# A prefetch hint for the closing branch of every engine's loop, in a four-layer transformer kernel

## The chip, the cores and the metric

The kernel runs on one core of a Trainium2 chip. The metric is the device time of one execution in microseconds (us), as the median of several runs. The core has five instruction streams that run side by side and meet only at semaphores: TensorE (PE in the profile; PEld is its weight load and PEq or PEldq its sequencer), VectorE (DVE), ScalarE (ACT), GpSimd (POOL) and SyncE (SP), which here issues the DMAs.

## The reference

Sixteen sequences of 512 tokens with 256 features pass through four pre-normalised residual layers. Cut to what matters:

```python
x = x + linear_attention(layernorm(x))      # L0 attention, 16 heads, phi = silu + 1
x = x + ternary_ffn(layernorm(x))           # L0 FFN: 256 -> 1024 gated, 1024 -> 1024 twice, 1024 -> 256
x = x + softmax_attention(layernorm(x))     # L1 attention, one head of 256
x = x + tanh(layernorm(x) @ W @ A1 @ A2 + bias)   # L1 FFN
```

`x` has the shape (16, 512, 256) in float32.

## The kernel before

One tile is one sequence. Its work is cut into steps with short names: A steps are the first attention, B, U, G, H and W the ternary FFN in two halves of 256 tokens, C and D steps the second attention and the last layer. `PLAN` (L128) writes out by hand one period in which three tiles are under way at once: the FFN of the tile in the middle (no prefix), the C steps of the tile before (`c:`) and the A steps and first FFN half of the tile behind (`a:`, `n:`). Each step says for every engine what it does; every engine walks the same list and does its own part of each step. A step's products run on PE, and the other engines empty PSUM banks, split values in a high and a low part, normalise and apply the functions. Two rings of four PSUM banks (`ffn_fill`, `att_fill`) and some fifty semaphores tie the engines together; a wait inside the loop compares with a register that is worked out from the iteration number.

`walk` (L322) lays out the program of PE, DVE, ACT and POOL alike: `PROLOGUE` and `FIRST` as straight code, then a loop of T - 2 = 14 iterations over `BODY`, which is `PLAN`, then `LAST` and `TAIL` as straight code. The loop is opened in L332. SP has a loop of its own (L435) of T - SLOTS = 12 iterations, which stores a finished tile and loads a new one.

The last step of a period is `W1`: on PE 32 products into one bank (L892), on DVE the scaling of that bank (L585) and the sum with `x` (L588). The first step is `U0`: on PE 16 products (L798) for two banks, on ACT a silu of the first (L728), on DVE the product of both (L570) and its rounded part (L575). Behind it in the list come `CST`, the statistics of the C layer on DVE (L505 to L512) with a power on POOL (L475), `U1` to `U3`, and `G0` (L834), whose last products need what POOL makes of `U3` (L488). Then follows `T`, the transposes in L850.

The products of the FFN stand twice in PE's program, once for weights that need full precision and once for those that don't, behind a branch on a flag that is read once (L817, L819). With these weights PE jumps over the first copy each time, 26 times in a period.

Of the kernel before, what the change touches and what calls it, by code (L numbers as in the profile page):

```python
# [41 lines left out]
T = 16  # L42
# [4 lines left out]
SLOTS = 4  # L47
# [162 lines left out]
def build(nc, a):  # L210
    with ExitStack() as ctx:
# [110 lines left out]
        def walk(eng, part):  # L322

            def steps_of(steps, counts, slots):
                for step in steps:
                    part(step, counts, slots)
                    counts.ahead(step)

            beginning = Counts(phases[0])
            steps_of(PROLOGUE, beginning, {"a": 0, "n": 0})  # L330
            steps_of(FIRST, beginning, {"": 0, "a": 1, "n": 1})
            with eng.Fori(0, T - 2) as it:  # L332
                steps_of(BODY, Counts(phases[2], rate, it),
                         {"c": eng.snap(it % SLOTS), "": eng.snap((it + 1) % SLOTS),
                          "a": eng.snap((it + 2) % SLOTS), "n": eng.snap((it + 2) % SLOTS)})
            steps_of(LAST, Counts(phases[3]), {"c": (T - 2) % SLOTS, "": (T - 1) % SLOTS})
            steps_of(TAIL, Counts(phases[4]), {"c": (T - 1) % SLOTS})
# [5 lines left out]
        def wait_apart(eng, which, value):  # L343

            if isinstance(value, int):
                eng.wait_ge(which, value)
            else:
                register = eng.to_reg(value)
                eng.wait_ge(consts, 7)  # L350
                eng.wait_ge(which, register)
# [13 lines left out]
        def wait_taken(eng, c, ring, k):  # L365

            b, n = c.bank(ring, k)
            eng.wait_ge(taken[ring][b], n)
# [17 lines left out]
        def km(name):  # L386
            return a[name].rearrange("(k p) n -> p k n", p=P)

        @block.sync
        def _(sp):  # L390
            sp.dma_start(x[:, 0], x_in[0]).then_inc(x_loaded, 16)
            sp.dma_start(raw_wkv[:, :, 0:D], km("wk0T")).then_inc(a_loaded, 16)
            sp.dma_start(raw_wkv[:, :, D:2 * D], km("wv0T")).then_inc(a_loaded, 16)
            sp.dma_start(raw_wq, km("wq0T")).then_inc(a_loaded, 16)
            sp.dma_start(wo[:], km("wo0T")).then_inc(a_loaded, 16)
            sp.dma_start(rows[:, 0:5, :], a["rows"][None].broadcast_to([P, 5, D])).then_inc(small_loaded, 16)
            sp.dma_start(cols[:], a["cols"]).then_inc(small_loaded, 16)
            sp.dma_start(scales[:], a["scales"]).then_inc(small_loaded, 16)

            parts = [[("w1T", w12[:, 0]), ("w2T", w12[:, 1])], [("h1T", h1[:])], [("h2T", h2[:])], [("w3T", w3[:])]]

            def bounce(layer):
                for name, _ in parts[layer]:
                    sp.dma_start(a["scratch_" + name], a[name]).then_inc(w_bounced[layer], 16)

            def land(layer):
                sp.wait_ge(w_bounced[layer], 16 * len(parts[layer]))
                for name, tile in parts[layer]:
                    sp.dma_start(tile.bitcast(F32), a["scratch_" + name].rearrange("(k p) n -> p k n", p=P))\  # L410
                      .then_inc(w_loaded[layer], 16)

            for tile, name in ((raw_q, "L1_attn_w_q"), (raw_k, "L1_attn_w_k"), (raw_v, "L1_attn_w_v"),
                               (raw_out, "woutT"), (raw_f, "wfT"), (raw_a1, "L1_ffn_aux_weight1"),
                               (raw_a2, "L1_ffn_aux_weight2")):
                sp.dma_start(tile, km(name)).then_inc(c_loaded, 16)
            bounce(0)
            bounce(1)
            land(0)
            land(1)  # L420
            bounce(2)
            land(2)
            bounce(3)
            land(3)

            c = Counts(phases[0])
            for step in PROLOGUE:
                if step[:2] == ("FOLD", 1):
                    wait_taken(sp, c, "att_fill", 2)
                c.ahead(step)  # L430
            for t in range(1, SLOTS):
                sp.dma_start(x[:, t], x_in[t]).then_inc(x_loaded, 16)
                sp.wait_ge(x_loaded, 16 * (t + 1))

            with sp.Fori(0, T - SLOTS) as t:  # L435
                slot = sp.snap(t % SLOTS)
                sp.wait_ge(s["out_ready"], t + 1)
                sp.dma_start(x_out[t], x[:, slot]).then_inc(x_stored, 16)
                wait_apart(sp, x_stored, 16 * t + 16)
                wait_apart(sp, x_loaded, 16 * t + 16 * SLOTS)  # L440
                sp.dma_start(x[:, slot], x_in[t + SLOTS]).then_inc(x_loaded, 16)
            for t in range(T - SLOTS, T):
                sp.wait_ge(s["out_ready"], t + 1)
                sp.dma_start(x_out[t], x[:, t % SLOTS]).then_inc(x_stored, 16)
            sp.wait_ge(x_stored, 16 * T)
# [3 lines left out]
        def _(pool):  # L449
# [28 lines left out]
            def part(step, c, slots):  # L478
# [11 lines left out]
                elif kind == "CF":  # L490
# [4 lines left out]
                    last.then_inc(s["out_ready"], 1)  # L495

            walk(pool, part)

        @block.vector  # L500
        def _(dve):
# [19 lines left out]
            def part(step, c, slots):  # L521
# [183 lines left out]
                elif kind == "CHECK":  # L705
                    bank, out = filled(dve, c, "att_fill", 0)
                    dve.tensor_reduce(flag[:, j:j + 1], bank[:, 0:2 * LOOKS[j]], AX.X, ALU.add).then_inc(out, 1)

            walk(dve, part)

        @block.scalar
        def _(act):
            def part(step, c, slots):
# [68 lines left out]
                elif kind == "PREP":  # L783
                    act.wait_ge(a_loaded, 16 * 4)
                    act.activation(wkv[0][:], raw_wkv, ACT.Copy).then_inc(s["split_hi"], 1)
                    act.activation(wq[0][:], raw_wq, ACT.Copy).then_inc(s["split_hi"], 1)

            walk(act, part)

# [265 lines left out]
```

## Time and profile before

| | us |
|---|---|
| median of 3 runs | 2127.78 |
| lowest and highest | 2126.31, 2128.02 |
| span of the profiled execution, first to last instruction | 2125.2 |
| median less that span | 2.6 |
| PE busy with products | 2016.7 (95% of the span) |
| DVE busy | 1208.1 (57%) |
| ACT busy | 837.6 (39%) |
| POOL busy | 373.5 (18%) |

The profiled execution has no time of its own beside its span; what lies around the span is therefore taken from the median. Register, branch and semaphore instructions are not counted as busy. They show in the trace with a q behind the engine's name. In the chain of waits, "issue" is time in which an engine waited for nothing that the profile shows.

### The profile page before, as it was taken

Reading aid. Unit: us, or ns where it says so; the run is one execution under the profiler, and the core shown is the slowest. Engines: PE = TensorE matmul, PEld = TensorE weight load, DVE = VectorE, ACT = ScalarE, POOL = GpSimd, SP = SyncE. Lnnn points to the kernel's source line nnn. Section 1 sums busy time; section 2 is a strip of 40 time slices with the busy share of each in tenths; the row PEclk is TensorE's granted clock in tenths of the full one; section 3 lists DMA queues with packets and bytes.
Section 4 is the critical chain, followed back from the end, with each engine's and each line's share of the span. In section 5 each row is a group of like instructions: output and inputs, shape, how many; then the busy total and the mean of one; then the engine's idle time right before and its main releaser. Section 6 shows DMA issues by size and latency. Waiting matters only on the chain.

```text
span 2125.2 us, 40501 instructions
## 1 busy us (share of the span) xinstructions
PE 2016.7 (95%) x15484; PEld 1938.4 (91%) x15484; DVE 1208.1 (57%) x2880; ACT 837.6 (39%) x1538; POOL 373.5 (18%) x347
## 2 busy tenths in 40 slices
PE   6899999999999999999999999999999999999985
PEld 5899999999999999999999999998999999999985
DVE  5556656465565645656365565655656466565544
ACT  2334434344443444434344343444434344343422
POOL 1111212012121011211012121121211112121011
PEclk9999999999999999999999999999999999999997
DMA  9400000000000000000000000000000000000000
GB/s 364 181 3 3 23 3 16 9 2 22 2 23 3 2 22 3 22 3 12 12 2 22 3 22 3 2 23 2 22 3 2 23 2 12 3 12 2 2 13 10
DMA packets 24567, 48.68 MB, mean 23 GB/s; under 512 B 1152, under 2 KB 21376, under 8 KB 24064
## 3 DMA queue, kind: packets, MB, share of 16 engines
q1 hardware_dynamic: 24240, 43.41, 5.8%
q8 instruction: 317, 5.19, 1.0%
q14 instruction: 10, 0.08, 0.0%
HBM read 35.02 MB, written 19.92 MB: 26 GB/s over the span
## 4 chain that ended last, share of the span: by engine, by line
PE 80%; DVE 6%; POOL 4%; issue 4%; ACT 3%; DMA 3%; SPq 0%; DVEq 0%; POOLq 0%; ACTq 0%
PE ffn_fill L834 43%; PE att_fill L798 23%; PE ffn_fill L892 6%; PE ffn_fill L798 5%; POOL act_lo L488 3%; PE att_fill L850 2%; DVE whole L570 2%; PE att_fill L968 1%; DMA scratch_h2T<-in_h2T 1%; DMA scratch_h1T<-in_h1T 1%; POOL rstd_C L475 1%; ACT L728 1%; ACT xt_hi L719 1%; DVE st L505 1%; DVE act_hi L575 1%
## 5 line engine op out<-in xcount | busy, mean ns | idle before, releaser
L834 PE MATMUL ffn_fill<-act_hi,h 128*128 128x256 f32 x4096 | 989.6, 284 | 9.2 <-POOL act_lo L488 3.5
L834 PE MATMUL ffn_fill<-act_lo,h 128*128 128x256 f32 x4096 | 980.6, 281 | 0.0
L834 PEld LDWEIGHTS ffn_fill<-act_hi,h 128*128 128x128 f32 x4096 | 773.5, 189 | 16.6 <-POOL act_lo L488 6.9
L834 PEld LDWEIGHTS ffn_fill<-act_lo,h 128*128 128x128 f32 x4096 | 774.6, 189 | 3.7
L579 DVE CAST act_hi<-whole 128x512 fp32r<-128x512 f32 x256 | 110.0, 430 | 572.0 <-ACT whole L737 572.0
L737 ACT ACTIVATE whole<-ffn_fill,scales 128x256 f32<-128x256 f32 x512 | 215.1, 472 | 556.5 <-PE ffn_fill L834 555.6
L798 PE MATMUL ffn_fill<-half_hi,w 128*128 128x256 f32 x1024 | 264.4, 297 | 40.6 <-issue 30.6
L798 PE MATMUL ffn_fill<-half_lo,w 128*128 128x256 f32 x1024 | 257.7, 290 | 0.0
L798 PEld LDWEIGHTS ffn_fill<-half_hi,w 128*128 128x128 f32 x1024 | 202.7, 198 | 47.6 <-issue 46.4
L488 POOL TENSOR_TENSOR act_lo<-whole,act_hi 128x512 fp32r<-128x512 f32 x128 | 166.6, 1301 | 410.9 <-DVE act_hi L575 410.3
L475 POOL TENSOR_TENSOR rstd_B<-var_eps_B,minus_half 128x2 f32<-128x2 f32 x32 | 22.6, 707 | 1131.5 <-DVE var_eps_B L512 1131.5
L798 PEld LDWEIGHTS ffn_fill<-half_lo,w 128*128 128x128 f32 x1024 | 203.1, 198 | 0.0
L581 DVE TENSOR_TENSOR act_lo<-whole,act_hi 128x512 fp32r<-128x512 f32 x256 | 190.9, 746 | 8.8
L737 ACT ACT_TABLE_LOAD x92 | 118.0, 1283 | 160.5 <-PE ffn_fill L834 144.3
L728 ACT ACTIVATE gated<-ffn_fill,scales 128x256 f32<-128x256 f32 x256 | 105.9, 473 | 165.9 <-PE ffn_fill L798 164.6
L570 DVE SCALAR_TENSOR_TENSOR whole<-ffn_fill,scales,gated 128x256 f32<-128x256 f32 x256 | 111.9, 479 | 76.3 <-PE ffn_fill L798 70.9
L892 PE MATMUL ffn_fill<-w,act_hi 128*128 128x256 f32 x512 | 123.9, 285 | 0.0
L892 PE MATMUL ffn_fill<-w,act_lo 128*128 128x256 f32 x512 | 121.2, 279 | 0.0
L892 PEld LDWEIGHTS ffn_fill<-w,act_lo 128*128 128x128 f32 x512 | 96.6, 189 | 0.0
L892 PEld LDWEIGHTS ffn_fill<-w,act_hi 128*128 128x128 f32 x512 | 96.1, 188 | 0.0
L505 DVE BATCH_NORM_STATS2 st<-x 128x6 f32 (+1 forms) x256 | 91.2, 414 | 7.2 <-DMA x<-in_L_attn_x 5.6
L470 POOL TENSOR_TENSOR x<-x,rows 128x512 f32 (+1 forms) x64 | 86.3, 1367 | 20.0 <-DVE xn L518 18.0
(155 smaller groups left out, 3155.0 us busy)
## 6 DMA issues: line engine op xcount, KB each, us to landing
x<-in_L_attn_x SPq DMA_DIRECT2D x16, 512.0 KB, 4.0
out<-x SPq DMA_DIRECT2D x16, 512.0 KB, 3.0
h<-scratch_h1T SPq DMA_DIRECT2D x1, 4096.0 KB, 16.2
h<-scratch_h2T SPq DMA_DIRECT2D x1, 4096.0 KB, 14.0
w<-scratch_w1T SPq DMA_DIRECT2D x1, 1024.0 KB, 14.6
w<-scratch_w2T SPq DMA_DIRECT2D x1, 1024.0 KB, 17.3
w<-scratch_w3T SPq DMA_DIRECT2D x1, 1024.0 KB, 5.8
rows<-in_rows SPq DMA_DIRECT2D x1, 640.0 KB, 6.3
```

Source lines behind the costliest of these rows:

```text
L470: last = pool.tensor_tensor(xs[:, b:b + 2, :], xs[:, b:b + 2, :], row2(bias_row), ALU.add)
L475: pool.tensor_tensor(rstd_of[stage][:, :nb], var_eps_of[stage][:, :nb], minus_half[:, :nb], ALU.pow)\
L488: pool.tensor_tensor(act_lo[0][:, blocks], whole[:, n % WHOLES], act_hi[0][:, blocks].bitcast(F32), ALU.subtract).then_inc(s["ffn_ready"], 1)
L505: last = dve.bn_stats(st[:, b, :], xs[:, b, :])
L570: last = dve.scalar_tensor_tensor(whole[:, n % WHOLES, o, :], two(bank)[:, o, :], scales[:, 1, 2 * j + o:2 * j + o + 1], gated[:, j % 2, o ...
L579: dve.tensor_copy(act_hi[dst][:, blocks], whole[:, n % WHOLES]).then_inc(s["hi_ready"], 1)
L581: dve.tensor_tensor(act_lo[dst][:, blocks], whole[:, n % WHOLES], act_hi[dst][:, blocks].bitcast(F32), ALU.subtract).then_inc(s["ffn_ready ...
L728: last = act.activation(gated[:, j % 2, o, :], two(bank)[:, o, :], ACT.Silu, scale=scales[:, 0, 2 * j + o:2 * j + o + 1])
L737: last = act.activation(whole[:, n % WHOLES, o, :], two(bank)[:, o, :], ACT.Gelu, scale=scales[:, layer, 2 * j + o:2 * j + o + 1])
L798: last = pe.matmul(out, lhsT, rhs, start=n == 0, stop=n == len(pairs) - 1)
L834: last = pe.matmul(two(bank)[:, o, :], view(w), view(moving[:, k, :]), start=k == 0 and o == 0 and half == 0, stop=k == KH - 1 and half == ...
L892: last = pe.matmul(two(bank)[:, b, :], view(part_of[:, k, b * P:(b + 1) * P]), view(w3[:, k, :]), start=k == 0 and b == 0 and half == 0, s ...
```

## The change

Both loops are opened through a form that takes one more argument, `hint_back_edge=True`. The loops run over the same range on the same engines. At the head of each iteration every engine gets one instruction, which names that engine's loop-closing branch and says that it is likely taken. Nothing else is added, taken out or moved.

```diff
@@ walk
-            with eng.Fori(0, T - 2) as it:
+            with nc.Fori(0, T - 2, engines=[eng.engine], hint_back_edge=True) as it:
                 steps_of(BODY, Counts(phases[2], rate, it),
@@ block.sync
-            with sp.Fori(0, T - SLOTS) as t:
+            with nc.Fori(0, T - SLOTS, engines=[sp.engine], hint_back_edge=True) as t:
                 slot = sp.snap(t % SLOTS)
```

In PE's program this is all that changes. The piece is the head of its loop: the end of `FIRST`, the entry, the hint, a register operation, and the flag's branch of `U0`.

```order
 L819 UNCONDITIONAL_BRANCH
 L332 UNCONDITIONAL_BRANCH
+L332 BRANCH_PREFETCH_HINT
 L332 ISA
 L817 COMPARE_AND_BRANCH
```

The hint is the first instruction of the iteration, and everything behind it stands one instruction later. From the hint to the closing branch PE's listing has 1,772 rows, of which nearly all are products; a product is a weight load and a matmul in the trace, so that the loop is some 3,500 instructions long.

On DVE it stands in the same way at the head of the loop, behind the last instruction of `W1` in the straight code.

```order
 L588 TENSOR_TENSOR x<-x,xn_b 128x512
 L332 UNCONDITIONAL_BRANCH
+L332 BRANCH_PREFETCH_HINT
 L332 ISA
 L341 ISA
```

Here too only the hint is new. By the same listing (which leaves out waits and register moves) the loops of DVE, ACT and POOL are 229, 87 and 49 rows long.

## Rows read from the trace of the kernel before

**Rows 1.** The page: engines, and the chain that ended last, by engine

```profile
PE 2016.7 (95%) x15484; PEld 1938.4 (91%) x15484; DVE 1208.1 (57%) x2880; ACT 837.6 (39%) x1538; POOL 373.5 (18%) x347
...
PE 80%; DVE 6%; POOL 4%; issue 4%; ACT 3%; DMA 3%; SPq 0%; DVEq 0%; POOLq 0%; ACTq 0%
```

**Rows 2.** Waits of PE: total us, times, longest us

```profile
PE ffn_fill L798 <- issue: 30.6, 15, 2.6
```

**Rows 3.** The loop's own instructions: duration in ns min/median/max, first and last start

```profile
L332 ACTq COMPARE_BRANCH  x14: 40/45/45, 284.3 to 1949.2; - x14
...
L332 PEldq COMPARE_BRANCH  x14: 76/3520/3893, 286.1 to 1950.9; - x14
...
L332 DVEq COMPARE_BRANCH  x14: 50/56/68, 288.8 to 1953.7; - x14
```

**Rows 4.** The same for SP's loop

```profile
L435 SPq COMPARE_BRANCH  x12: 44/45/54, 242.0 to 1650.8; - x12
```

**Rows 5.** The same, one back edge alone, 285 to 292 us

```profile
L332 PEldq COMPARE_BRANCH  x1: 3297/3297/3297, 286.1 to 286.1; - x1
L332 DVEq ALU_OP  x1: 40/40/40, 288.7 to 288.7; - x1
L332 DVEq COMPARE_BRANCH  x1: 68/68/68, 288.8 to 288.8; - x1
L332 DVEq FUSED_REGOPS  x1: 63/63/63, 289.2 to 289.2; - x1
L332 PEldq FUSED_REGOPS  x1: 50/50/50, 289.4 to 289.4; - x1
```

**Rows 6.** DMA from 287 to 288 us: queue, packets, MB, share

```profile
q8 instruction: 1, 0.02, 6.0%
```

**Rows 7.** Chain of work, loop entered from straight code: start, us, what

```profile
159.24 3.74 PE ffn_fill L892 x32
162.98 1.90 PE ffn_fill L798 x16
...
164.91 0.02 DVEq L362
...
165.10 0.89 DVE whole L570 x2
...
174.87 1.22 PE ffn_fill L834 x8
176.08 0.87 PE att_fill L850 x8
```

**Rows 8.** Chain of work at the first back edge

```profile
287.95 1.97 issue
289.92 3.07 PE ffn_fill L798 x16
...
302.98 1.21 PE ffn_fill L834 x8
304.19 0.87 PE att_fill L850 x8
```

**Rows 9.** Chain of work, end of the last iteration, exit to straight code

```profile
1949.07 3.74 PE ffn_fill L892 x32
1952.81 1.91 PE ffn_fill L798 x16
```

**Rows 10.** Stretches: length, busy us (instructions) of PE, PEld, DVE, ACT, POOL, clock, DMA

```profile
162.98:176.08 13.10, 11.98 (x99) 11.54 (x98) 11.06 (x27) 4.64 (x9) 6.66 (x6) 1.00 0.01 3
287.95:304.19 16.24, 13.68 (x99) 13.27 (x99) 11.05 (x27) 4.65 (x9) 6.68 (x6) 0.89 0.01 3
...
289.92:295.30 5.38, 5.38 (x32) 5.38 (x33) 2.06 (x6) 1.55 (x4) 0.68 (x1) 0.68 0.01 3
```

**Rows 11.** PE's flag branches, 60 to 80 us, then 160 to 1955 us: ns min/median/max

```profile
L817 PEldq COMPARE_BRANCH  x4: 218/1757/3918, 61.5 to 75.5; - x4
...
L817 PEldq COMPARE_BRANCH  x366: 200/224/463, 161.6 to 1953.7; - x183
```

**Rows 12.** Waits of PE, 60 to 80 us: total us, times, longest us

```profile
PE ffn_fill L834 <- issue: 2.3, 2, 1.7
```

## The prediction

> **What bounds the kernel now.** I read the page first: PE is busy for 2016.7 of 2125.2 us and the chain that ended last is 80% PE [rows 1]. So a branch can only matter where PE itself runs dry. The next view is the list of PE's waits. Its longest entry is no wait for another engine but "issue", 30.6 us in 15 pieces of up to 2.6 us, ahead of the products of a U step [rows 2]. U0 is the first step of an iteration, and 14 iterations have 13 taken back edges; that fits. The third view is the loop's own line. PE's closing branch is there 14 times, with a median of 3520 ns and a minimum of 76 ns, while the same branch takes 40 to 68 ns on DVE, ACT and POOL [rows 3] and 44 to 54 ns on SP [rows 4]. The minimum is the fourteenth, which is not taken: it began at 1950.9, and behind it PE goes from W1 into the straight code with no gap, 1949.07 + 3.74 = 1952.81 [rows 9]. The thirteen taken ones are the long ones.
>
> One edge in detail shows why. PE's branch begins at 286.1 and takes 3.297 us; the next instruction is at 289.4 [rows 5]. In that time a single packet of 16 KB moves on the instruction queue, in the microsecond from 287 to 288 [rows 6]. PE still had products in its queue and finished W1 at 287.95; then it stands for 1.97 us [rows 8]. On DVE the branch takes 0.068 us and the next instruction starts 0.3 us later [rows 5], with no such fetch. So the code at the head of the loop is on DVE still at hand when the branch comes, and on PE, whose loop of 3,500 instructions is by far the longest, it has to be brought.
>
> **What an edge costs.** The loop's first iteration is entered from straight code, without a back edge, and runs the same steps; it is the measure of a free edge. From the end of W1 to the transposes behind G0 it takes 13.10 us there, 162.98 to 176.08, and 16.24 us at the first back edge, 287.95 to 304.19 [rows 7, 8]. That is 3.14 us, more than the gap of 1.97. The rest is the clock: the granted clock is 1.00 in the first stretch, and 0.68 from 289.92 to 295.30 [rows 10], that is, behind the gap PE works for a while at 1.2 instead of 2.4 GHz, and U0 takes 3.07 us instead of 1.90 [rows 7, 8]. A part of that is swallowed, since the way from U0 over DVE and POOL to G0 has some slack of its own.
>
> For all 13 I take periods, from the end of one loop-closing W1 to the next. The first is 287.95 - 162.98 = 124.97 us, without an edge in it. The 13 others, each with one taken edge at its start, take 1952.81 - 287.95 = 1664.86 us, or 128.07 each [rows 7, 8, 9]. The difference is 3.10 us per edge and 40.2 us in all.
>
> **The change, part by part.** (1) PE's hint. If it does what it says, the code at the loop's head is there when PE's sequencer reaches the branch, and the branch costs what it costs on DVE: 0.07 us and 0.3 to the next instruction. The sequencer is ahead of the array at that place: it reaches the branch at 286.1, PE finishes W1 at 287.95, a lead of 1.85 us. From the branch's end at 289.4 to the first product at 289.92 another 0.52 us pass [rows 5, 8]. So the branch and the hint behind it may together take 1.85 - 0.52 = 1.33 us before PE feels anything. Taken with 0.4 us for the branch, that leaves 0.9 us for a hint. PE then has no gap, and without a gap no slower clock, as at the loop's entry, where the clock stayed at 1.00. The term is -40.2 us.
>
> (2) The hint's own time, 14 times on each engine. No hint is in this trace. The nearest rows are the loop's register operations, 0.05 us on PE and 0.063 on DVE; the far end is the longest flag branch in the loop, 0.463 [rows 5, 11]. I take 0.05 to 0.1 us as the row of the same kind. On PE it lies under the lead just worked out. On DVE it lies ahead of U0's product: at the entry DVE took up its wait for this at 164.91, 1.93 us after the end of W1 [rows 7]; at the back edge its sequencer is through with the branch and at the next instruction at 289.2, 1.25 us after W1 [rows 5, 8]. The margin is 0.7 us, which takes either end. ACT and POOL have passed their branches 3 us and more before W1 ends [rows 3], and SP waits for a finished tile most of the time. All of these are 0; if the DVE margin were gone, each tenth beyond it would cost 1.3 us over 13 edges. Both ends for the whole: 0 and +2.
>
> (3) The loop's exit. There the hint is wrong once. If the head's code has been brought instead of the code behind the loop, PE pays one on-demand fetch, as an edge does now: 3.1 us. The other end is 0, since the branch not taken cost 76 ns and the code behind it was there [rows 3, 9]. I take 0.3.
>
> (4) Everything behind the hint stands one instruction later. The flag branches, taken 26 times in an iteration over some 32 to 64 instructions, stay under 0.463 us in the whole loop [rows 11]; one place more or less should keep it so. 0.
>
> Sum: -40.2 + 0.3, or -39.9. Against the profiled span of 2125.2 this is 2085.3. The median of the runs is 2.6 us above that span, which gives **2087.9 us**, 1.9% less. The span is one execution, and the three runs lie 1.7 us apart, so the terms are good to about 1 us plus their own bounds. The 13 edges agree well enough to be scaled: the branch's median is 3.52 and its maximum 3.89 us [rows 3]. The full case is 2084 to 2093. What is late next, once the edge is free, is the way from U0 over DVE's statistics and POOL to G0: the first iteration has it, and it is in the 124.97 us.
>
> **The rivals.** *The hint changes nothing on PE.* Between the hint and its branch lie some 3,500 instructions, many fetches of 16 KB, and 26 taken flag branches without hints. If any of these makes the fetch unit forget what it was told, or if it only ever brings what comes next, the branch stays at 3.5 us. For it speaks that nothing in this trace shows code being brought ahead of a taken branch to a far place; against it, that the branch not taken is served in 76 ns, so that fetching ahead does work along this code. Time: 2127.8, or up to 2 more. Chance 0.12. The Trainium skill, "Runtime: NRT & Kernel Launch", section on instruction fetch mechanics, calls the prefetch "purely sequential" and says that a taken branch to a target outside the two pages at hand forces a fetch before execution goes on. Its second part the trace bears out, with 3.3 to 3.9 us; by its first part the hint would be without effect, and the time this rival's.
>
> *Half a cure.* The fetch starts ahead of the branch but too late, or the hint's work itself is dear, and a part of the 3.5 us remains beyond the 1.33 that are hidden. With half of the gap left, about 1.1 us on each edge, and less of the slow clock, 15 to 20 us of the 40 stay: 2103 to 2108. Against it: while PE runs W1 alone, 3.74 us, there is more time than the branch takes now. Chance 0.10.
>
> *Slower: the hinted code takes another's place.* Room for code is limited, else PE's head would still be there. If the block that the hint brings in pushes out, or goes ahead of, the block that comes next in the body, a flag branch or a plain step inside each iteration has to wait for its code. That this costs something can be seen before the loop: two flag branches of up to 3.918 us there, with 2.3 us of issue on PE [rows 11, 12]. One such miss in each of 14 iterations at an edge's price of 3.1 us is +43. If the back edge becomes free as well, the two cancel and the time is 2131 with a wrong exit; if it does not, 2171. The point from which it decides is 13 misses: fewer, and the change gains. In the loop as it is there is no flag branch over 0.463 us, which speaks for slack in the fetches. Chance 0.07, in which the time is over 2132.
>
> **How the numbers follow.** Chances: full case 0.71, half a cure 0.10, nothing 0.12, slower 0.07. A difference of 0.2%, about 4 us, is what a measurement of this kernel can tell. Faster takes the full case and the half: 0.81. Same: 0.12. Slower: 0.07. The range has to reach from the full case through the half cure: 2083 to 2110, which leaves 0.19 out.
>
> **What would show it.** Right: PE's 13 taken closing branches at well under 1.3 us; no "issue" ahead of U0; U0 at 1.9 us and the granted clock at 1.00 behind each edge; about 125 us from W1 to W1; DVE's branch unchanged. The exit branch and what follows it show term 3. Wrong: closing branches still at 3.3 us and more (rival one), long flag branches in the body or new issue gaps ahead of L834 (rival three), or a DVE product of U0 that starts more than 2.2 us after W1 (term 2).

## The result, and the profile after

| | before | after |
|---|---|---|
| median of 20 runs each, us | 2128.12 | 2130.36 |
| lowest and highest, us | 2124.45, 2131.2 | 2126.15, 2137.27 |
| ratio, 95% interval | | 1.0013 [1.0007, 1.0019] |
| span of the profiled execution, us | 2125.2 | 2128.1 |

The change does not pay. It costs about a thousandth of the time, inside the 0.2% that the prediction called "same", and 40 us from the forecast of 2087.9. The page of the kernel after reads as before [rows 1]:

```profile
PE 2017.7 (95%) x15484; PEld 1940.3 (91%) x15484; DVE 1207.4 (57%) x2880; ACT 837.5 (39%) x1538; POOL 373.9 (18%) x347
...
PE 80%; DVE 6%; issue 4%; POOL 4%; DMA 3%; ACT 2%; SPq 0%; DVEq 0%; POOLq 0%; ACTq 0%
```

The longest wait of PE is still there, with the same count [rows 2]:

```profile
PE ffn_fill L798 <- issue: 31.5, 15, 2.6
```

The loop's own instructions (ns min/median/max, first and last start in us) show the hint on every engine, and show that PE's closing branch did not get shorter [rows 3, 4]:

```profile
L332 POOLq BRANCH_PREFETCH_HINT  x14: 31/31/43, 154.8 to 1818.3; - x14
...
L332 PEldq BRANCH_PREFETCH_HINT  x14: 45/45/45, 161.3 to 1828.3; - x14
...
L332 DVEq BRANCH_PREFETCH_HINT  x14: 39/39/61, 164.1 to 1827.5; - x14
...
L332 ACTq COMPARE_BRANCH  x14: 44/49/68, 284.5 to 1952.0; - x14
...
L332 PEldq COMPARE_BRANCH  x14: 85/3636/3803, 286.3 to 1953.8; - x14
...
L332 DVEq COMPARE_BRANCH  x14: 55/61/84, 289.0 to 1956.5; - x14
```

The chain of work at the first back edge has the same gap behind W1 [rows 8]:

```profile
284.39 3.74 PE ffn_fill L892 x32
288.13 2.44 issue
290.57 2.18 PE ffn_fill L798 x16
```

And the instruction queue, from 278.2 us to 286.2, the moment at which that branch begins (40 slices of 0.2 us, a digit where a packet starts, then the count of packets):

```profile
DMA  0000002000000000000000000000000000000000
...
q8 instruction: 1, 0.02, 0.7%
```

One fetch at 279.5, and then nothing for almost seven microseconds up to the branch. The next starts at 287.3, a microsecond into the branch, as in [rows 6]. In both kernels there are 317 fetches in all, 20 from one closing branch to the next. So the hint was executed 14 times and nothing was fetched on its account ahead of the branch.

**Where the small loss comes from.** From the end of one W1 to the next, the 13 periods with an edge take (1955.65 - 288.13) / 13 = 128.27 us, against 128.07 before: 0.20 us each, 2.6 in all. Behind a branch that is not hidden, nothing is hidden: from the hint at 290.0 to the register operation at 290.1 the sequencer needs 0.1 us more than before, while PE stands.

```profile
L332 PEldq COMPARE_BRANCH  x1: 3654/3654/3654, 286.3 to 286.3; - x1
...
L332 PEldq BRANCH_PREFETCH_HINT  x1: 45/45/45, 290.0 to 290.0; - x1
L332 PEldq FUSED_REGOPS  x1: 50/50/50, 290.1 to 290.1; - x1
```

That is 1.3 us over 13 edges, about half of the loss. The taken branches themselves, which vary between 3.3 and 3.9 us in either kernel, sum to 46.8 us here against 46.3 before, another 0.5. What is left is not assigned, and no run carries the hints of the other engines alone.

### The profile page after: what moved, and what is told of

Read it like the earlier page. It is cut to its first block, busy times and chain, and to the rows that moved or that the text cites. A ratio compares the mean times of both kernels' runs of the same rounds, so it can differ in the third digit from the quotient of the medians.

```text
span 2128.1 us, 40569 instructions
## 1 busy us (share of the span) xinstructions
PE 2017.7 (95%) x15484; PEld 1940.3 (91%) x15484; DVE 1207.4 (57%) x2880; ACT 837.5 (39%) x1538; POOL 373.9 (18%) x347
## 4 chain that ended last, share of the span: by engine, by line
PE 80%; DVE 6%; issue 4%; POOL 4%; DMA 3%; ACT 2%; SPq 0%; DVEq 0%; POOLq 0%; ACTq 0%
PE ffn_fill L834 43%; PE att_fill L798 22%; PE ffn_fill L892 6%; PE ffn_fill L798 5%; POOL act_lo L488 3%; DVE whole L570 2%; PE att_fill L850 2%; PE att_fill L968 1%; DMA scratch_h2T<-in_h2T 1%; DMA scratch_h1T<-in_h1T 1%; POOL rstd_C L475 1%; DVE st L505 1%; DVE act_hi L575 1%; ACT L728 1%; DMA h<-scratch_h2T 1%
## 5 line engine op out<-in xcount | busy, mean ns | idle before, releaser
L798 PE MATMUL ffn_fill<-half_hi,w 128*128 128x256 f32 x1024 | 266.0, 298 | 43.0 <-issue 31.5
L798 PE MATMUL ffn_fill<-half_lo,w 128*128 128x256 f32 x1024 | 259.0, 291 | 0.0
L798 PEld LDWEIGHTS ffn_fill<-half_hi,w 128*128 128x128 f32 x1024 | 203.8, 199 | 49.5 <-issue 48.7
L798 PEld LDWEIGHTS ffn_fill<-half_lo,w 128*128 128x128 f32 x1024 | 204.0, 199 | 0.0
```

What stands on the lines that cost most here:

```text
L798: last = pe.matmul(out, lhsT, rhs, start=n == 0, stop=n == len(pairs) - 1)
```

## The experiments

All full-computation kernels below differ from the kernel before only in PE's loop; those of the last group that have a hint keep the hints of the other engines as well. In the kernels whose hint does not stand at the head, the loop is written by a helper that does what `Fori` does and puts the hint where a mark stands in the code. "Fetch" means a packet of 16 KB on the instruction queue. How many instructions one brings can be read from noflag2_head below, where PE runs through all of its loop: 4,011 instructions in the trace of an iteration and 16 fetches, 251 each. It is taken as 256 instructions of 64 bytes, called a block here. By the compiled program PE's loop with its hint is 4,899 instructions from head to closing branch, 19 blocks and 35, which fits the 20 fetches of an iteration; the prediction's count of 3,500 had left out that a full-precision product is four instructions. All times are medians; "one run" means a single time. The kernel before, run beside them, gave single times from 2122.6 to 2132.1 us over all chips, so a single time can tell 40 us, barely 10, and not 3. Where a single time is all there is, the argument rests on the lengths of its 6 or 13 closing branches.

### Is the price of the edges right?

**pe_straight**: PE's 14 periods written out one behind the other, no loop on PE, the other engines keep theirs.

```diff
-            with eng.Fori(0, T - 2) as it:
-                steps_of(BODY, Counts(phases[2], rate, it),
+            straight(steps_of, phases[2], rate) if eng.engine == mybir.EngineType.PE else None
+            for it in opened(eng, T - 2): steps_of(BODY, Counts(phases[2], rate, it),
```

> PE's 14 periods written out as straight code, no loop and no back edge on PE; the other engines keep their loops. This prices the edges themselves, apart from any hint: 13 edges at 3.10 us each, so 2128.1 - 40 = 2088 (2084 to 2094), with no issue gap ahead of U0. If the code written out costs fetches of its own, or registers had hidden something, it lies above 2094.

Measured: 2086.69 us, ratio 0.9803 [0.9787, 0.982]. At the place of the first back edge U0 follows W1 at once:

```profile
284.43 3.74 PE ffn_fill L892 x32
288.17 1.90 PE ffn_fill L798 x16
```

The 13 edges cost 41 us, where the prediction had 40.2. The term was right; what failed is the hint.

### Is the hint too far ahead, or lost at a flag branch?

Between the hint at the head and its branch lie 26 taken flag branches and 19 fetches. Three kernels carry the hint nearer to the branch:

```diff
-                    emit(lambda ap: ap)
+                    mark(pe, c, "else"); emit(lambda ap: ap)
...
+PLACES = [('H', 3, 'else', 2)]
```

**h3_else** puts it into the second H3, behind that step's flag branch, with only W1's flag branch left between; **h3_ahead** ahead of H3's flag branch; **w1_else** behind W1's, with no taken branch between.

> PE's hint alone, moved from the head of the loop to the last H3 of the period, inside the copy of its products that is executed, so behind H3's own flag branch; one flag branch (W1's) and two plain branches lie between it and the closing branch. Three theories. Forgetting at any flag branch: W1's flag branch voids it, closing branches stay at 3.3 to 3.9 us and the time at 2128 to 2130, unless the fetch has already been started by then, which happens if the block that holds the closing branch is entered between the hint and W1; the last fetch ahead of the branch was 7.2 us before it, while H3 was under way, so in that case the branches fall under 0.5 us and the time to 2086 to 2092. Distance (a hint 128 us ahead of its branch is too early): the same 2086 to 2092, since 9 us are left. Hints never work on PE: 2128 to 2130, closing branches at 3.5 us.

> The same hint a few instructions earlier: directly ahead of H3's flag branch instead of directly behind it. If a flag branch voids a hint, closing branches are at 3.5 us here and the time is 2128 to 2130, whatever the run before it shows. If only distance matters, it is as good as the run before it: 2086 to 2092 and branches under 0.5 us.

> PE's hint inside the executed copy of W1, behind the last flag branch of the period, some 70 instructions and about 3 us ahead of the closing branch. No flag branch follows, so forgetting would let it work if the fetch still starts when the block is already entered: branches at 0.1 to 1.5 us, time 2086 to 2105. If the fetch unit decides only on entering a block, the hint comes too late: branches at 3.5 us, 2128 to 2130. Never: 2128 to 2130.

Measured: 2128.26 us, ratio 1.0003 [0.9994, 1.0013]; 2125.79 and 2129.4 (one run each). The closing branches, in this order:

```profile
L1089 PEldq COMPARE_BRANCH  x14: 85/3505/3736, 286.9 to 1951.4; - x14
```
```profile
L1089 PEldq COMPARE_BRANCH  x14: 85/3466/3879, 286.2 to 1949.8; - x14
```
```profile
L1089 PEldq COMPARE_BRANCH  x14: 85/3430/3836, 288.0 to 1953.6; - x14
```

None helps. Even 3.7 us ahead with nothing in between, about the time that the branch needs on demand (3.3 to 3.8 us), the hint does nothing. So it is not its distance alone, and in w1_else there was no flag branch to lose it at.

I then laid the loop's head at a fixed place, instruction 10 of a block, with the hint at H3 and without any:

```diff
+    if SLOT is not None:
+        eng.addr_align(bass.FETCH_BLOCK_INSTRUCTIONS, offset=SLOT, max_nops=0)
     nc.br(start_name, engines=engines)
```

> The hint stands behind H3's flag branch as before, but the loop's head is laid to place 10 of a block of 256 instructions, so that the block which holds the closing branch begins some 180 instructions ahead of it: behind the hint (217 ahead) and before W1's flag branch (140 ahead). Voiding theory (any flag branch that is executed makes a hint void, and the fetch unit looks at the hint when it enters a block): for the first time nothing lies between the hint and the entry, so the 13 closing branches fall from 3.5 us to under 0.5, and the time to 2086 to 2092. Theory that hints don't work on PE at all: 3.5 us and 2128 to 2130.

> The same layout with no hint anywhere: the control for the layout. Closing branches at 3.5 us, 2126 to 2130, by both theories. If the branches are short here, the layout did it and not the hint.

> The same layout with the hint directly ahead of H3's flag branch, 283 instructions before the closing branch, so well before the entry, but with one flag branch between. Voiding theory: closing branches at 3.5 us, 2128 to 2130. If what counts is only that the hint comes before the entry of the block, it is as good as behind the flag branch: 2086 to 2092.

Measured: 2126.18 us, ratio 0.9996 [0.9983, 1.0009]; 2129.26 and 2125.66 (one run each); closing branches at medians of 3.47, 3.41 and 3.53 us. The three did not separate anything. They read as if place did not matter, which was a wrong conclusion from one place only, as the last group shows.

### Does it work in another body?

**noflag2_head** has no flag branches in PE's loop (the copies of the products for weights that need full precision are left out there), two periods in an iteration and the hint at the head; **noflag2_none** is the same without the hint. Both have 6 taken back edges. Below are the line that leaves the copies out, and the one in which the two differ.

```diff
+                if c.it is not None: return emit(lambda ap: ap)
...
-PLACES, SLOT, AT_TOP = [], None, True
+PLACES, SLOT, AT_TOP = [], None, False
```

> PE's loop without flag branches (the copy of the FFN products for weights that need full precision is left out in the loop) and with two periods in an iteration, some 3,970 instructions, so that it is longer than the loop of the change; the hint stands at the head, as in the change. There are 6 taken back edges instead of 13. Voiding theory: the hint holds over 3,900 instructions and some fifteen blocks, closing branches under 0.5 us, 2086 to 2092. Distance theory or no effect on PE: six branches at 3.5 us, six edges at 3.1 us, so 2104 to 2109.

> The loop of two periods without flag branches, this time without a hint: the control for the run that came out at 2086.4 with closing branches of 0.36 us. The copy of the FFN products for weights that need full precision is left out in the loop. If the hint did the work there, the 6 taken branches are at 3.3 to 3.9 us here and the time is 2104 to 2109. If it was the shorter code or the lack of flag branches, nothing changes: 0.36 us and 2086 to 2088.

Measured, one run each: 2086.4 and 2096.55 us. The hint is worth 10 us over 6 edges, and the closing branches, with it and without:

```profile
L1093 PEldq COMPARE_BRANCH  x7: 88/357/358, 411.5 to 1907.5; - x7
```
```profile
L1093 PEldq COMPARE_BRANCH  x7: 83/3482/3890, 410.1 to 1921.2; - x7
```

So the hint does what it says, over 4,000 instructions. The control still missed its 2104 to 2109: an edge is worth less in total than the 3.1 us that the expectation took. From one closing branch to the next it is worth 2.5 us ((1921.2 - 410.1) / 6 = 251.85 against (1907.5 - 411.5) / 6 = 249.33), 15 us in all. The kernel with the hint is 1.4 us later before its first back edge and loses 3.6 us behind the loop. Of these, 1.9 us are a wait that noflag2_none does not have, four products behind the loop's exit, the one place where the hint is wrong:

```profile
1909.36 0.47 PE ffn_fill L798 x4
1909.83 1.86 issue
```

My theory was then that a flag branch on the way voids it. Three kernels tested that. **last4_h1** takes the flag branches (and the full-precision copies) out of the last four steps only, H1, H2, H3 and W1, and hints ahead of H1, so that no branch lies between; **last4_head** is the same code with the hint at the head and 22 flag branches between; **last4_w1flag_h1** hints ahead of H1 but keeps W1's flag branch.

```diff
+                if bare(c): return emit(lambda ap: ap)
...
+PLACES, SLOT, AT_TOP, BARE = [('H', 1, 'ahead', 2)], None, False, [('H', 1, 2), ('H', 2, 2), ('H', 3, 2), ('W', 1, 1)]
```

> One period per iteration and all the flag branches of the change but the last four (H1, H2, H3 in the second half and W1, whose full-precision copy is left out); PE's hint stands directly ahead of H1, about 275 instructions before the closing branch, so that no flag branch follows it and at least one block of 256 instructions is entered behind it. Voiding theory: the 13 closing branches fall to about 0.36 us, 2086 to 2092. If hints work only in a loop free of flag branches: 3.5 us and 2126 to 2130.

> The same code as the run before it with the hint at the head of the loop, as in the change, and so ahead of the 22 flag branches that are left. Voiding theory: closing branches at 3.3 to 3.9 us, 2126 to 2130. If only a flag branch close to the end or after the entry of the last block did harm: 0.36 us, 2086 to 2092.

> As the hint ahead of H1, but W1 keeps its flag branch and both copies: one flag branch between hint and closing branch. Voiding theory: 3.5 us and 2126 to 2130 if the last block is entered behind that branch, under 0.5 us and 2086 to 2092 if it is entered ahead of it and the fetch is under way. With the full-precision copy of W1 the closing branch lies 140 instructions and more behind W1's flag branch, so the place of the entry decides; a fetch in the DMA rows between 12 and 8 us before the closing branch and none 1 us after it would show the second.

Measured, one run each: 2126.1, 2101.88 and 2089.01 us. The closing branches in this order:

```profile
L1098 PEldq COMPARE_BRANCH  x14: 85/3492/3773, 286.3 to 1950.1; - x14
```
```profile
L1098 PEldq COMPARE_BRANCH  x14: 93/2116/2701, 287.7 to 1926.5; - x14
```
```profile
L1098 PEldq COMPARE_BRANCH  x14: 85/459/473, 288.1 to 1913.0; - x14
```

The theory fell, and from both sides: the kernel without a branch behind the hint fails, the ones with one and with 22 succeed in full or in part. The instruction queue shows what tells them apart. Here are the 8 us up to the first closing branch, in slices of 0.2 us, of last4_h1, last4_head and last4_w1flag_h1:

```profile
DMA  0000000000000000000000000000000000000000
```
```profile
DMA  0000000000000000000000000000000000000030
```
```profile
DMA  0000000000000000000000000400000000000000
```

No fetch: 3.5 us. A fetch 0.35 us ahead: 2.4 us left at this edge (2.1 at the median). A fetch 2.9 us ahead: 0.46 us. The branch is as long as its fetch is late: over the 13 edges of last4_head the fetch starts between 1.3 us ahead of the branch and 0.3 us behind its start, and the branch ends 2.3 to 2.9 us after the fetch starts each time, as it does where the fetch starts on demand, 1.0 us into a branch of 3.3 to 3.9. And the fetch at -2.9 us comes 1.1 us behind W1's flag branch, which in that kernel jumps to a place not entered before (it takes 0.36 us; inside the same block it takes 0.23). That led to the theory of place: **the target's fetch starts only when PE's sequencer has come into the block that holds the closing branch**, whenever the hint itself was executed. The next group bears it out where the block is entered by a jump, and leaves it open where it is entered by running on.

### The place in the block

These kernels are the change itself, whole computation, hint at the head, plus one argument that says at which instruction of a block PE's loop begins. The closing branch is 35 instructions further on in its own block.

```diff
-            with nc.Fori(0, T - 2, engines=[eng.engine], hint_back_edge=True) as it:
+            with nc.Fori(0, T - 2, engines=[eng.engine], hint_back_edge=True, head_slot={eng.engine: 100} if eng.engine == mybir.EngineType.PE else None) as it:
```

> The change as it is, whole computation, with one argument more on PE's loop: its head is laid at instruction 100 of a block of 256 instructions (the instruction queue fetches 256 instructions, 16 KB, at a time in the trace). The body is 4,899 instructions, 19 blocks and 35, so the closing branch should come near instruction 135 of its block instead of near its beginning. Theory of place (the target is fetched ahead only if the block that holds the closing branch is entered long enough before the branch): nearly all closing branches of line 332 under 0.6 us, the fetch of the target one to four us before them, and 2086 to 2092 us. Theory that something in the body that all layouts with the full-precision copy share voids the hint: branches stay at 3.3 to 3.9 us, 2125 to 2131 us.

> The same place of PE's loop head (instruction 100 of a block) without any hint. Both theories: closing branches 3.3 to 3.9 us, 2124 to 2130 us. If the place alone shortened the back edge, the branches would be short here too, and the theory of place would be about the layout and not about the hint.

> As slot100_head with the head at instruction 40, the closing branch thus near instruction 75 of its block. Theory of place: graded, the branch comes about one quarter of a block after its block is entered, so the branches lie between 0.4 and 2 us and the time between 2086 and 2110 us. Theory of something shared in the body: 3.3 to 3.9 us, 2125 to 2131 us.

> As slot100_head with the head at instruction 200, the closing branch thus near instruction 235 of its block: it is late in its block. Theory of place: under 0.6 us, 2086 to 2092 us, the fetch of the target several us ahead. Theory of something shared in the body: 3.3 to 3.9 us, 2125 to 2131 us.

> The change as it is with PE's loop head laid at instruction 10 of a block. In slot40_head and slot100_head the last flag branch of the body (line 817, ahead of W1's products) takes 0.44 us, as those do that jump into a block not entered before, and a fetch, that of the hinted target, follows it by 1.1 us, 2.8 us before the closing branch. With the head at 10 all places move back by 30, that jump should stay inside the block it comes from, and the closing branch's block is entered by running on, too late. Theory of place: branches 3.3 to 3.9 us, 2124 to 2130 us, no fetch in the five us before them. If the fixed head alone mends it (a moved label of the loader, say), 0.44 us and 2086 to 2089 us.

> The same with the head at instruction 25, fifteen instructions short of slot40_head. Theory of place: if the last flag branch still jumps into the closing branch's block, 0.44 us and 2086 to 2089 us; if it falls short of it, that block is entered by running on, and the branches lie between 1 and 3.9 us, the time between 2098 and 2130 us. In either case the length of that flag branch (0.44 or 0.23 us) and the length of the closing branch go together.

Measured (slot100_head in 4 runs, ratio 0.9818 [0.9801, 0.9835]; the others one run each):

| head at | hint | time, us | last flag branch, us | last fetch ahead of the closing branch | closing branch, median us | issue ahead of U steps (L798), us |
|---|---|---|---|---|---|---|
| 10 | yes | 2132.25 | 0.23 | 7.2 us | 3.38 | 30.1 |
| 25 | yes | 2130.62 | 0.23 | 7.2 us | 3.49 | 30.2 |
| 40 | yes | 2086.19 | 0.42 | 2.8 us | 0.44 | none listed |
| 100 | yes | 2087.35 | 0.35 | 2.9 us | 0.44 | 2.0 |
| 100 | no | 2121.21 | 0.42 | 2.9 us | 3.40 | 34.2 |
| 200 | yes | 2124.95 | 0.24 | 5.1 us | 0.45 | 27.2 |

The flag branch and the fetch are those of one edge, the third for the head at 200 and the first for the others. Of the expectations, those of slot10_head, slot25_head and slot100_none missed their times by 0.6 to 2.8 us (single times) and met their branches, slot40_head came in at the best end of a wide range, and slot200_head missed.

Fifteen instructions of padding, from 25 to 40, are worth about 44 us, one run each. The flag branch ahead of W1, the last of the body, and under it the instruction queue in the 8 us up to the first closing branch, first with the head at 25, then at 40:

```profile
L817 PEldq COMPARE_BRANCH  x1: 232/232/232, 285.4 to 285.4; - x1
```
```profile
DMA  0002000000000000000000000000000000000000
```
```profile
L817 PEldq COMPARE_BRANCH  x1: 422/422/422, 281.8 to 281.8; - x1
```
```profile
DMA  0000020000000000000000000030000000000000
```

At 25 that jump takes 0.23 us, which is read as staying in the block it comes from, and no fetch follows. At 40 it takes 0.42 us and is read as landing in the next one, the block of the closing branch. The count agrees: W1's executed copy is 64 instructions, and the closing branch stands some 60 (head at 25) or 75 (head at 40) into its block. At 40 the fetch follows 1.2 us later, 2.8 us before the closing branch, and the branch takes 0.42 us. The two go together as the expectation of slot25_head put it.

With the head at 100 the same fetch is seen with and without the hint. The 8 us up to the first closing branch, and all branches of L332, of slot100_head and then of slot100_none (15 of them, since the jump over the padding ahead of the loop is counted too):

```profile
DMA  0000200000000000000000000200000000000000
```
```profile
L332 PEldq COMPARE_BRANCH  x15: 85/441/456, 162.2 to 1910.8; - x15
```
```profile
DMA  0003000000000000000000000200000000000000
```
```profile
L332 PEldq COMPARE_BRANCH  x15: 76/3404/3936, 159.7 to 1945.3; - x15
```

Without the hint, what is fetched at that moment does not help the back edge; with it, the branch is short. The fetches from the first closing branch to the second show that the hint replaces one and adds none. Without it there are 21, since the target has to be fetched on demand besides; with it there are 20:

```profile
q8 instruction: 21, 0.34, 1.1%
```
```profile
q8 instruction: 20, 0.33, 1.0%
```

The reading nearest to this is that on coming into a block PE fetches one further block, the next in order, and that the hint changes which one. What a packet holds the trace does not say, so this is inferred from the lengths of the branches. The place alone does not shorten the back edge: slot100_none has all its 13 long branches. The same control for the head at 40 was not run.

**slot200_head** is the miss worth looking at. Its closing branches are short, 0.45 us, and yet it gains nothing. At the third back edge, the closing branch, the flag branch behind it, and the chain of work:

```profile
L332 PEldq COMPARE_BRANCH  x1: 447/447/447, 544.2 to 544.2; - x1
...
L332 PEldq BRANCH_PREFETCH_HINT  x1: 45/45/45, 544.7 to 544.7; - x1
```
```profile
L817 PEldq COMPARE_BRANCH  x1: 2618/2618/2618, 545.1 to 545.1; - x1
```
```profile
544.92 1.17 PE ffn_fill L892 x10
546.09 1.66 issue
547.75 2.18 PE ffn_fill L798 x16
```

The next taken branch, U0's flag branch, stands a few instructions behind the head and jumps over the full-precision copy, 16 products or some 64 instructions, out of the head's block, of which only 56 instructions were left. So the hint seems to have brought the head's block and no other. The stall has moved from the closing branch to the flag branch, 0.45 us later. From 160 to 1955 us there are 15 flag branches over a microsecond, 13 behind the back edges, one in the first iteration and one behind the exit, and none over 0.5 in the change or with the head at 40. All flag branches of that stretch, of slot200_head and of the kernel after [rows 11]:

```profile
L817 PEldq COMPARE_BRANCH  x367: 207/233/3392, 163.0 to 1952.4; - x184
```
```profile
L817 PEldq COMPARE_BRANCH  x365: 207/232/472, 161.8 to 1954.2; - x183
```

With the head at 100 it begins to show: 14 flag branches, U1's, take 0.8 to 1.7 us there, of which PE's queue covers all but the 2.0 us of the table. 40 is the better place.

## Why the prediction was wrong

**The step that failed is term (1)**, in its first sentence: "the code at the loop's head is there when PE's sequencer reaches the branch". It took for granted that a hint executed 120 us ahead is acted on in time, wherever the loop lies. In this body it was not acted on at all ahead of the branch: no fetch in the last 7 us, and the branch at 3.64 us instead of 3.52. What decides is the place of PE's loop in its blocks of 256 instructions: with the same hint the branch takes 3.4 to 3.5 us with the head at instruction 10 or 25 of a block, and 0.44 at 40 or 100. The rival "the hint changes nothing on PE" gave 2127.8 "or up to 2 more", and that is in effect what came, 2130.36 against 2128.12, 2.2 more. It had a chance of 0.12. Both reasons I gave for it were wrong, though: neither a flag branch nor the 19 fetches between make the fetch unit forget the hint (last4_head works in part through 22 flag branches, slot40_head in full through all 26), and it does not only bring what comes next. The rule of the Trainium skill that stood beside it (page "Runtime: NRT & Kernel Launch", on instruction fetch mechanics: prefetch is "purely sequential") gives the right time here for the wrong reason, by luck of the layout; noflag2_head, slot40_head and slot100_head show that a hinted target is fetched ahead.

**What was right in the same term.** The price of an edge, 3.10 us and 40.2 in all: pe_straight gains 41, and in slot100_head the 13 periods from W1 to W1 take 124.90 us each, where the entry's free period had been 124.97:

```profile
285.25 3.74 PE ffn_fill L892 x32
288.99 1.90 PE ffn_fill L798 x16
...
1908.90 3.74 PE ffn_fill L892 x32
1912.64 1.89 PE ffn_fill L798 x16
```

(1912.64 - 288.99) / 13 = 124.90. The estimate of 0.4 us for the cured branch measured 0.44, it is hidden under the 1.33 us of lead, and the granted clock stays at 1.00, the 2.4 GHz level, behind the edge, as forecast. The stretch from W1's end to the transposes, which took 13.10 us at the entry and 16.24 at the edge [rows 10], is now, in slot100_head (length, busy us of the engines, clock, DMA):

```profile
288.99:302.12 13.13, 11.90 (x99) 11.51 (x98) 11.06 (x27) 4.63 (x9) 6.69 (x6) 1.00 0.01 2
```

slot40_head came in at 2086.19, slot100_head at 2087.35, against the 2087.9 forecast for the full case.

**Term (2), the hint's own time.** 45 ns on PE, 39 on DVE, 31 on the others, below the 0.05 to 0.1 that I took from the register operations. It is hidden where the branch is short. In the change, where it is not, PE's stall is 0.1 us longer at the edge shown, because the cover named for it, the lead, is what the long branch uses up.

**Term (3), the exit.** 0.3 us was taken; the last closing branch, not taken, takes 85 ns in the change and in slot100_head, and W1 is followed by U0 at once (1908.90 + 3.74 = 1912.64 above). In the change that makes 0. It is not 0 wherever the hint works: behind the exit PE stands 0.71 us after U0 in slot100_head and 1.86 us in noflag2_head, where slot100_none and noflag2_none have no such wait, and 0 again in slot40_head. The mechanism of the term, a fetch spent on the head when the code behind the loop was needed, fits these; its size lay within the bounds of 0 and 3.1.

**Term (4), one place more or less for everything behind the hint: 0.** This held for one place (no flag branch of the change takes over 0.472 us), and the sentence was still the one to stop at. The jumps are also longer than the 32 to 64 instructions that it gave, 64 to 128 by the count of four for a product. Places decide here: 15 of them turn nothing into 44 us, and with the head at 200 a flag branch of the body takes 2.6 us and more in each period. That is also the third rival's mechanism in a form that I had not thought of. I expected the hinted block to push another out; instead the block behind the head is late. Its arithmetic was good: one such miss per iteration cancels the free edge, and slot200_head stands at 2124.95.

**Half a cure** is what last4_head shows: target fetched too late, about 2.1 us of branch left, 2101.88, a little under its 2103 to 2108.

No run says how the natural place of the change compares with the numbers of the table; its fetches, its last flag branch (0.23 us) and its branches are those of the heads at 10 and 25. The single times of these two, 0.3 and 1.9 us above the change's median, are within its lowest and highest.

## What to carry to other kernels

A hint for a loop's back edge is only half of the remedy for a body that has to be fetched: also say where the loop lies. Look at three things in the trace: the length of the closing branch; how far ahead of it the last fetch starts, beside the same kernel without the hint (the one 7.2 us ahead in slot25_head did not bring the target); and whether one of the first taken branches behind the head or behind the exit has become long. The version with the head at instruction 40 of a block does the whole computation with one argument more, 2086.19 us in its one run, and that at 100 has 0.9818 [0.9801, 0.9835] of the time before; writing the loop out gives the same at 14 times the code.

And when a change consists of telling the hardware something, ask the trace of before for a row in which the hardware does that thing at all. There was none, I said so, and still gave it 0.12.

## What the runs showed of the hardware that I had not expected

- A hint takes 31 to 45 ns on its engine and is remembered over 120 us, 19 fetches and 26 taken branches (slot40_head, slot100_head).
- The fetch of a hinted target does not start where the hint is executed. Where a flag branch jumps into the closing branch's block, it starts 1.1 to 1.7 us after that jump: in slot40_head and slot100_head, whose hint stands 124 us ahead, and in last4_w1flag_h1, whose hint stands 15.9 us ahead and whose fetch is 2.3 to 2.9 us ahead.
- From the start of a fetch to the end of the branch that waits for it pass 2.3 to 2.9 us, ahead of the branch or on demand (last4_head and the kernel before).
- PE's taken branches fall into groups: 0.20 to 0.26 us, 0.31 to 0.51, and 2.2 to 3.9, with some between (slot100_head, last4_head). They are read as a jump inside a block, one into a block at hand, one into a block that is not, and one whose fetch is under way. The count of instructions agrees for W1's flag branch with the head at 25 and 40; by this reading the lengths mark block boundaries in a trace.
- The closing branch itself became 4 to 5 ns longer with the hint (DVE 56 to 61 ns, ACT 45 to 49 [rows 3]).
- Padding alone changes which branches wait: slot100_none has 330 fetches against 317, 34.2 us of issue against 30.6, and 13 flag branches of 2.2 to 2.8 us. Its time is no longer for it, 2121.21 us in one run.
